# Attention, gated MLP and recurrence on one core: the softmax shift moves into a spare row of the third score product, and the next batch's first maximum work moves ahead of the last heads' sums

## The reference, cut to what matters

```python
xn = _layernorm(x)                                  # x: 4 batches, 1024 tokens, 128 features
# first layer, attention branch
k = xn @ Wk.T; q = xn @ Wq.T; v = xn @ Wv.T
e = einsum('biq,bjq->bij', q, k @ Wa.T)             # 1024 x 1024 scores a batch, no scale
s = softmax(e, axis=-1) @ (v @ Wb.T)
# first layer, MLP branch
h = silu((xn @ w1.T) * s1) * ((xn @ w2.T) * s2)     # 512 hidden
h = gelu((h @ h1.T) * c1); h = gelu((h @ h2.T) * c2)
x = x + s * silu((h @ w3.T) * s3)
# second layer: a recurrence over tokens in 8 heads, and a 16-head attention with 8 experts
x = x + s2nd(xn2) * silu(moe_and_attention(xn2))
```

## Time and profile before

| | |
|---|---|
| median of 3 runs | 1000.63 us (1000.05 to 1000.78) |
| the profiled execution | 999.73 us |
| its span | 997.9 us, 20056 instructions |
| PE, ACT, DVE, POOL busy | 96%, 74%, 55%, 20% |
| granted PE clock, mean | 0.992 |

### The profile page before, as it was taken

How to read it: one execution, slowest core, us unless ns; L and a number is a source line. 1 busy time by engine, 2 the same in 40 slices (tenths; PEclk the granted TensorE clock), 3 DMA queues, 4 the chain that set the end, 5 groups by cost and what they waited for, 6 DMA issues and landing times.

```text
span 997.9 us, 20056 instructions
## 1 busy us (share of the span) xinstructions
PE 953.5 (96%) x8050; PEld 538.2 (54%) x8050; DVE 551.2 (55%) x1342; ACT 742.0 (74%) x915; POOL 195.0 (20%) x142
## 2 busy tenths in 40 slices
PE   4999999999899999999989999999999999999996
PEld 3788643343388863334358884334436887433431
DVE  6655735645456654564565574456447467356354
ACT  5543699989763379998956449999895436999886
POOL 1200202522210020340230002134122003024122
PEclk9899999999999999999999999999999999999998
DMA  6000133000000023200000012310000001320000
GB/s 252 1 1 1 21 48 67 1 3 2 1 22 1 1 36 49 51 2 2 2 22 1 0 14 40 50 34 1 2 1 22 1 1 20 48 46 2 2 2 24
DMA packets 17649, 22.31 MB, mean 22 GB/s; under 512 B 2992, under 2 KB 14352, under 8 KB 17296
## 3 DMA queue, kind: packets, MB, share of 16 engines
q1 hardware_dynamic: 17552, 20.99, 10.4%
HBM read 7.85 MB, written 2.10 MB: 10 GB/s over the span
## 4 chain that ended last, share of the span: by engine, by line
PE 75%; ACT 10%; DVE 8%; issue 6%; POOL 1%; DMA 0%; DVEq 0%; ACTq 0%; POOLq 0%
PE ps L1135 74%; ACT big L1086 6%; DVE st L280 1%; ACT xn L1058 1%; DVE wk L747 1%; ACT spl L1039 1%; DVE wk L571 1%; DVE mx L492 1%; PE ps L1155 1%; POOL st L898 1%; DVE xn L460 0%; DVE spl L468 0%; ACT qz L1034 0%; DVE flags L428 0%; DMA xnext<-in_x 0%
## 5 line engine op out<-in xcount | busy, mean ns | idle before, releaser
L1086 ACT ACTIVATE big<-ps 128x1024 f32<-128x1024 f32 x512 | 491.0, 1042 | 35.9 <-PE ps L1135 35.4
L1135 PE MATMUL ps<-big,vaug 128*32 128x512 f32 x2048 | 272.6, 604 | 3.8 <-DVE wk L747 2.3
L1135 PE MATMUL ps<-hid 32*128 32x512 f32 x1024 | 130.6, 492 | 5.8 <-ACT big L1086 4.0
L1135 PE MATMUL ps<-hid,fw_sb 128*128 128x512 f32 x416 | 101.2, 397 | 0.3 <-DVE hid L476 0.3
L1002 ACT ACTIVATE wk<-ps,cols_sb 128x512 f32<-128x512 f32 x64 | 40.5, 687 | 80.2 <-PE ps L1135 74.4
L898 POOL TENSOR_TENSOR st<-st 128x4 f32<-128x4 f32 x16 | 16.2, 1010 | 388.1 <-DVE st L560 288.0
L1135 PEld LDWEIGHTS ps<-hid 32*128 32x128 f32 x1024 | 49.3, 181 | 78.8 <-issue 43.0
L912 POOL TENSOR_TENSOR qz<-qz,wk 128x512 f32<-128x512 f32 x32 | 41.2, 1287 | 237.8 <-DVE wk L717 237.8
L1135 PEld LDWEIGHTS ps<-hid,fw_sb 128*128 128x128 f32 x416 | 77.5, 188 | 18.5 <-DVE hid L476 1.1
L1135 PEld LDWEIGHTS ps<-big,vaug 128*32 128x32 f32 x2048 | 41.1, 108 | 70.1 <-issue 36.5
L735 DVE SCALAR_TENSOR_TENSOR big<-ps,sm,big 128x128 f32<-128x128 f32 x128 | 44.2, 345 | 46.7 <-PE ps L1135 36.0
(11 more groups left out here) (221 smaller groups left out, 1577.2 us busy)
## 6 DMA issues: line engine op xcount, KB each, us to landing
hid<-spl SPq DMA_DIRECT2D x288, 32.0 KB
xnext<-in_x SPq DMA_DIRECT2D x4, 512.0 KB, 4.0
big<-in_fw SPq DMA_DIRECT2D x1, 1877.0 KB, 8.8
out<-qz SPq DMA_DIRECT2D x7, 256.0 KB, 2.3
hid<-one_row SPq DMA_DIRECT2D x16, 96.0 KB
wk<-in_lw SPq DMA_DIRECT2D x1, 1476.0 KB, 13.7
big<-in_fw SPq DMA_DIRECT2D x1, 939.0 KB, 10.7
cst_sb<-in_cst SPq DMA_DIRECT2D x1, 440.0 KB, 4.4
```

The lines of the kernel that those rows point to most:

```text
L1086: up(ms_exp, a.activation(prob[:, at:at + 2 * CH].rearrange("p (h n) -> p h n", n=CH), ps[:, bank:bank + 2, :], ACT.Exp, scale=HDM ** -0.5))
L1135: return t_.matmul(out_, lhsT, rhs, start=start, stop=stop, **kw)
```

## The change

The change has three parts.

**A row less in r, and the shift in it.** The last feature's column is subtracted from all columns of the first factor product ("Wa Wk"), so that the last row of r is exactly zero; since a layer-normed x sums to zero over its features, the scores stay the same. The last row of `spl[:, 1]` is then free, and the DMA writes the shift there. The third product of a score unit takes `x_one` in place of `xt_hi` as its stationary operand: a copy of rows 0 to 126 of `xt_hi` with ones in row 127, held in `spl[:, 2]`. So that product adds the shift, and the fourth product falls away, as do POOL's memsets of `shift`. `x_one` is made by three SP DMAs a batch: two of 127 rows by 512, one of the row of ones; the score stage waits for all of them (`x_one_in`).

**Work moved ahead.** For batches 1 to 3, `row_scores(0)`, `row_maximum(0)` and the value products 0 to 3 stand in the batch before, in front of the last "nat" and in "r" 1. The remaining row scores and value products are woven anew.

**DVE's gates.** The split halves of `gate_unit(0, m)` come one or two gates later.

```diff
-        negrow, shift = spl[0:1, 2, :], spl[:, 2, :]
+        negrow, x_one = spl[P - 1:P, 1, :], spl[:, 2, :]
...
+            sp.wait_ge(x_lo.sem, 2)
             sp.wait_ge(wide_ok, 1)
             wide = sp.value_load(iflag[0:1, 0:1], min_val=0, max_val=1)
...
+            def key_rows(c):
+                sl = slice(c * CH, (c + 1) * CH)
+                return sp.dma_start(x_one[0:P - 1, sl].bitcast(F32), xt_hi[0:P - 1, sl].bitcast(F32))
+
+            def ones_in_last_row():
+                return sp.dma_start(x_one[P - 1:P, :].rearrange("p (a n) -> p a n", n=P).bitcast(F32),
+                                    one_row[0:1, :].bitcast(F32).unsqueeze(1).broadcast_to([1, S // P, P]))
+
+            for c in range(NCH):
+                up(x_one_in, key_rows(c), 16)
+            up(x_one_in, ones_in_last_row(), 16)
...
                 if b < B - 1:
                     up(x_in, load_x(b + 1), 16)
+                    for c in range(NCH):
+                        sp.wait_ge(x_hi.sem, x_hi.at(b, 3 + c))
+                        up(x_one_in, key_rows(c), 16)
+                    up(x_one_in, ones_in_last_row(), 16)
...
-            done(v.tensor_copy(xn[:, 5 * D:6 * D], ps[:, 0, 0:D]), "Wa Wk")
+            done(v.tensor_copy(mrow[:, :], ps[:, 0, D - 1:D]))
+            so_far()
+            done(v.tensor_scalar(xn[:, 5 * D:6 * D], ps[:, 0, 0:D], mrow[:, 0:1], None, ALU.subtract), "Wa Wk")
...
-                for m in range(KM):
-                    gate_unit(0, m)
+                gate_unit(0, 0)
+                gate_unit(0, 1)
+                gate_split(0, 0)
+                gate_unit(0, 2)
+                gate_split(0, 1)
+                gate_unit(0, 3)
+                gate_split(0, 2)
+                gate_split(0, 3)
...
                     elif what == "nat":
+                        if i == 2 * NG - 1 and b < B - 1:
+                            row_maximum(0, b + 1)
                         attention_out(i)
...
-                up(shift_zero, g_.memset(shift.bitcast(I32), 0))
...
+                def u_unit(t):
+                    ins = split3(ps[:, 4 + t // TPC, (t % TPC) * D:(t % TPC + 1) * D], *tok(t), gh_hi[:, D:2 * D], gh_lo[:, D:2 * D])
+                    if t % TPC == TPC - 1:
+                        up(u_mm, ins)
...
-                    split3(ps[:, SC_BANKS[n_], :], *tok(jt), spl[:, 0, sl], spl[:, 1, sl], True, False)
+                    with_high(ps[:, SC_BANKS[n_], :], *tok(jt), spl[:, 0, sl])
...
+                t_.wait_ge(x_one_in.sem, x_one_in.at(b, 48))
                 t_.wait_ge(negrow_in.sem, negrow_in.at(b, 16))
...
-                    up(sc_mm, mm(ps[:, SC_BANKS[n_], :], one_row[:, :], shift[:, h * CH:(h + 1) * CH], False, True))
+                    up(sc_mm, mm(ps[:, SC_BANKS[n_], :], x_one[:, jt * P:(jt + 1) * P], spl[:, 1, h * CH:(h + 1) * CH], False, True))
...
                     elif what == "nat":
+                        if i == 2 * NG - 1 and b < B - 1:
+                            t_.wait_ge(r_hi.sem, r_hi.at(b, 1))
+                            row_scores(0)
+                            u_unit(2)
+                            u_unit(3)
...
                         if i:
+                            u_unit(0)
+                            u_unit(1)
                             t_.wait_ge(r_lo.sem, r_lo.at(b, i))
```

More of the change, by code:

```diff
@@ L225, in build_program @@
         maxT, neg_ok, negrow_in = sig("maxT"), sig("neg_ok"), sig("negrow_in", 16)
-        shift_zero = sig("shift_zero", 1, 1)
+        x_one_in = sig("x_one_in", 48)
         l1_mm, l1_act, hid_hi, hid_lo = sig("l1_mm", 16), sig("l1_act", 8), sig("hid_hi", 24), sig("hid_lo", 24)
@@ L332, in _ @@
                     weight_blocks(b, 0, 2)
-                sp.wait_ge(shift_zero.sem, shift_zero.at(b, 0))
                 sp.wait_ge(neg_ok.sem, neg_ok.at(b, 1))
@@ L485, in gate_unit, with gate_split, row_maximum @@
                     up(gated, v.scalar_tensor_tensor(h_, ps[:, L1_BANKS[c][m % 2] + 1, :], col("w2s", m), h_, ALU.mult, ALU.mult))
+                def gate_split(c, m):
+                    n_ = c * KM + m
                     v.wait_ge(gated.sem, gated.at(b, n_ + 1))
                     split_hidden(n_, 2 * c, m)
-                def row_maximum(t):
-                    v.wait_ge(max_mm.sem, max_mm.at(b, t + 1))
+                def row_maximum(t, of=b):
+                    v.wait_ge(max_mm.sem, max_mm.at(of, t + 1))
                     bank = MAX_BANKS[t % 2]
                     up(row_max, v.tensor_reduce(mx[:, t:t + 1], ps[:, bank:bank + 2, :], AX.XY, ALU.max))
-                for t in range(NT):
+                for t in range(NT) if b == 0 else range(1, NT):
                     row_maximum(t)
@@ L551, in _ @@
                     gate_unit(1, m)
+                    gate_split(1, m)
                 act_units(0, 8, 1)
@@ L883, in _ @@
             g_.memset(half, -0.5).then_inc(half_set, 1)
-            g_.memset(shift.bitcast(I32), 0).then_inc(shift_zero.sem, 1)
             g_.wait_ge(half_set, 1)
@@ L1192, in row_scores @@
                     ins.then_inc(max_mm.sem, 1)
+                def u_unit(t):
+                    ins = split3(ps[:, 4 + t // TPC, (t % TPC) * D:(t % TPC + 1) * D], *tok(t), gh_hi[:, D:2 * D], gh_lo[:, D:2 * D])
+                    if t % TPC == TPC - 1:
+                        up(u_mm, ins)
                 t_.wait_ge(r_hi.sem, r_hi.at(b, 0))
-                row_scores(0)
+                if b == 0:
+                    row_scores(0)
                 t_.wait_ge(oT_ok.sem, oT_ok.at(b, 0))
@@ L1198, in _ @@
                 row_scores(1)
[L1199 to L1204, removed]
+                for t in range(NT) if b == 0 else range(TPC, NT):
+                    u_unit(t)
+                    if b and t in (5, 7):
+                        row_scores(2 + (t - 5) // 2)
                 if b == 0:
@@ L1276, in first_layer @@
                     l1_unit(0, 0, general)
+                    if b:
+                        row_scores(4)
+                        row_scores(5)
+                    t_.wait_ge(u_ok.sem, u_ok.at(b, 2))
+                    if b:
+                        l1_unit(0, 1, general)
                     row_scores(6)
-                    t_.wait_ge(u_ok.sem, u_ok.at(b, 2))
-                    l1_unit(0, 1, general)
+                    if b == 0:
+                        l1_unit(0, 1, general)
                     row_scores(7)
@@ L1308, in _ @@
                         score_products(n_)
-                    h = n_ // NT
+                    h, jt = n_ // NT, n_ % NT
                     if b == 0 and n_ == 13:
```

## The result

The changed kernel takes 1011.61 us (median of 4 runs, 1010.95 to 1012.29), against 1000.7 for the kernel before on the same chip: a ratio of 1.0106, 95% interval 1.0094 to 1.0118. It is 10.9 us slower; the forecast was 17.9 us slower. The profiled execution took 1010.95 us, with a span of 1009.1 us and a mean granted clock of 0.985 (before 0.992).

What follows compares the result with a forecast made beforehand. PE, busy 96% of the span, was taken as the bound, with DVE's maxima as much so before the transpose. Stalls 25.7 plus clock 8 less gains 15.8 gave +17.9 on 1000.63: 1018.5 us, range 984 to 1067.

Steps and rivals of the forecast that it cites:

- The price's mechanism: The `x_one` DMAs on SP's queue: each 127-row copy runs on one engine and the score stage waits, 25.7 us of stalls.
- The first rival: The `x_one` copies spread over many engines and come in time, leaving the whole gain: 984.8 us, chance 0.15.
- T: Time of one 127-row `x_one` copy on one engine: 11.4 us, taken between the weight loads' pace and the store's.
- The forecast's own sum: Change of the whole kernel's time: stalls plus clock less gains, 8T - 73.3, or +17.9 us.
- stall, batch 0: PE's wait before batch 0's closing products for copies and shift row: 2T - 11.2, or 11.6 us.
- stalls, batches 1 to 3: PE's wait before each later batch's closing products for copies, stores and shift row: 2T - 18.1, or 4.7 us.
- the clock: PE's clock falls to its lower level in the score stage after each stall: 2 us each, 8 in all.
- gains: Fourth product dropped and work moved ahead: 3.24 us for batch 0, 4.2 for each later batch, 15.8 in all.
- the formulas: PE's stalls before the closing products: 2T - 11.2 in batch 0, 2T - 18.1 in each later batch.
- The queue behind the copies: On the copies' engine in batches 1 to 3: its share of two stores, 1.8 us, then the shift row, 0.3 to land.
- 2.78: Score stage: twelve units inside it each lose a matmul of 0.232 us, saving 2.78 us a batch.
- 1.41: Ahead of the score stage, batches 1 to 3: the first units can be closed 1.41 us earlier, at 524.34 instead of 525.75.

Runs made afterwards that it cites:

- e1_spread: The changed kernel with each 127-row copy cut into one of 112 rows and one of 15: 982.21 us.
- e8_stores_later: The changed kernel with a batch's two stores issued behind the next batch's shift row instead of ahead of it: 1004.7 us.
- e7_gates_back: Against e1_spread, DVE's gates in the old order, each product split right away: 985.36 us.
- e4_extra128: The changed kernel with a third copy a batch, of 128 rows, into a buffer that nothing reads: 1014.97 us.
- e3_extra127: The changed kernel with a third copy a batch, of 127 rows, into a buffer that nothing reads: 1052.68 us.
- e2_half_spread: The changed kernel with only the copy of columns 0 to 511 cut into 112 and 15 rows: 985.72 us.
- e9_early_first: The changed kernel with batch 0's three DMAs for `x_one` issued ahead of SP's read of `iflag`: 997.28 us.

## Why the prediction was right in its sign and too high in its size

**The price's mechanism held.** Each copy ran on one engine, with one completion. One engine is what the Trainium skill (DMA: Bandwidth & Descriptors, "Why a DMA increments its semaphore by 16 and not by 1") says of 127 partitions, and this case's trace agrees. The first rival, the spread copy at 984.8 us, was wrong for this kernel and came within 2.6 us of the one that cuts the copies.

**The term that was mis-sized is T.** I chose 11.4 us between the loads' 10.4 and the store's 13.8. It measured 11.2 for the first copy and 10.2 for the one behind it, together 21.3 us or 10.7 each, near the loads' end. The forecast's own sum says what that does: four times 21.3, less 73.3, is +11.9, and +10.9 was measured. The agreement to 1 us is partly luck, as the terms show:

| term | predicted, us | measured, us |
|---|---|---|
| stall, batch 0 | 11.6 | 9.34 |
| stalls, batches 1 to 3 | 4.7 each | 3.2 each |
| the clock | 8 | 7.9 (2.2, 1.3, 1.7, 2.7 by batch) |
| gains | 15.8 | 18.2 |
| sum | +17.9 | +8.7 from these rows; +10.9 by time |

The clock's term is the difference of the score stages' lengths to `e1_spread`, whose clock is full there; the 2 us a stall was a choice between 0 and 4.5, and that the four differ so much and still add up to nearly 8 is luck. With 21.3 us for the two copies the formulas give 10.1 for batch 0 and 3.2 for the others, against 9.34 and 3.20. In batch 0 two errors nearly cancel: the closing came at 52.65 where the formula has 51.1, and PE was ready at 43.3, not 41.0. The queue behind the copies was right too. On the same engine stand the two copies, that engine's share of the stores (1.8 predicted, 1.4 by `e8_stores_later`), and the shift row.

The upper end of the stated range, 1078, does not come out of these terms: T = 18 gives 1071. Nothing here hangs on it.

**The gains were undersized by 2.4 us** (18.2 by `e1_spread`). The closings of the profiled executions of before and `e1_spread`, which lie 17.5 us apart, say where.

- From the first to the last closing a score stage is 2.9 us shorter (11.83 and 8.90 in batch 2), where 2.78 was forecast, since matmuls stand 0.227 apart and not 0.232: 0.5 us more in four batches.
- From the last closing of a batch to the first of the next it is 2.0, 1.7 and 2.4 us shorter, where 1.41 was forecast: 1.9 us more. The transpose is the part that was mis-sized: in batch 2 it came 1.37 earlier, not 0.95. Why the other two batches gained more still is not shown.
- The first closing of batch 0 is not 0.46 earlier as forecast, but 0.4 later.

In batch 2 of `e1_spread` this makes 4.6 us (closing to closing 236.18, before 240.79), where the forecast had 4.2. The sentence that the gates' new order keeps `gated` ahead of PE held: PE waits for no gate in `e1_spread`. The forecast put no number on that order, and `e7_gates_back` shows that 3.2 us of the gains hang on it, since the old order would have fallen behind PE's new pace. It is no part of the 2.4, as the forecast had PE running without a gap.

**What the table lacks.** Its sum is 2.2 us short of the measured 10.9. 1.4 lie ahead of the first closing of batch 0, where PE is ready at 43.3 and in `e1_spread` at 41.9. From PE's second group of products at 11.68 up to 33.4 us the two traces run alike within 0.02 us, though the first load landed 1.2 us later in the run of after. Then in the run of after 512-column matmuls stand 0.43 us apart up to 36.6 us, as they do behind the stalls, where the granted clock is 0.50; in `e1_spread` they stand 0.23 apart from 34.8 on. The windows give a granted clock of 1.00 for this stretch in both runs, so it has to be read from the matmuls. No edit touched it, and why the faster pace came later there is not shown. 0.7 is the profiled execution's distance from its median, and 0.3 lie in the rest of the span; these three cover the difference.

## What to carry to other kernels

Before a DMA is put on a path that something waits for, count its rows: a copy of 127 partitions ran on one engine and took 10 to 11 us; one such copy was still hidden here, the second was not, and cut into 112 and 15 rows both were. The completions counted as packets under 512 bytes told the number of engines in every trace here (1, 8, 15 and 16). When a stage is made shorter, look again at the engine that feeds it: an order that was in time for the old pace may be late for the new one.

## What the runs showed of the hardware that was not expected

- SP's queue itself was held. With two copies outstanding on the one engine, the next DMA took 10.11 us to issue, whatever it was: a 4 KB row, or in `e4_extra128` a copy of 128 rows (10.10). In `e3_extra127` two such holds followed each other, 10.12 and 10.11 us, each ending some 2 us behind the completion of a copy. With one copy outstanding, in `e2_half_spread`, the same 4 KB row took 3.67 us, and with both copies cut up, in `e1_spread`, 0.67. The hold cost nothing more here: the stores go out 3.9 us ahead of the transpose in the kernel after (527.37 and 531.29) and 4.0 in `e1_spread`, which has no hold. I had counted on issues that cost SP nothing but their turn.
- A short stall can cost the clock as well, or not. Behind 3.2 us of idle PE the score stage took 1.3, 1.7 and 2.7 us longer in three batches of one run, and in `e9_early_first` once nothing; behind some 1.85 us in `e8_stores_later` it took 1.6 us longer twice and once nothing. Behind 9.34 us it took 2.2 longer, so the price does not follow the length of the stall.
- Kernels that differ only later in the program differ by up to 4 us in when PE is ready for the first closing (41.9 in `e1_spread`, 45.7 in `e2_half_spread`), by where the clock is low at the start. A single profile does not resolve a term smaller than that there.
